# A message-passing loop whose routing work on VectorE is issued in parts of two to four operations over several steps

## The reference

```python
agg = segment_sum(feature[src] * alpha[:, None], dst)
x = x + agg @ W_fc.T + b_fc + mix(layernorm(x))
h = layernorm(x)
probs = softmax(h @ gate_w + gate_b)
idx = argmax(probs); prb = probs[idx]
one_hot = one_hot(idx, E)
pos = (cumsum(one_hot, axis=0) * one_hot).sum(-1) - 1
kept = pos < C
buf[idx, where(kept, pos, C)] = h          # then two matmuls per expert
y = ybuf[idx, min(pos, C - 1)] * prb * kept
```

## Time and profile before

| | |
|---|---|
| median of three runs | 2648.24 us (2640.82 to 2654.11) |
| span of the profiled execution, first to last instruction | 2181.3 us |
| the median less the span | 466.9 us |
| VectorE busy, whole span | 1486.4 us (68%) |
| TensorE busy | 1899.4 us (87%) |
| GpSimd busy | 1223.5 us (56%) |
| ScalarE busy | 781.6 us (36%) |
| window 1201 to 1757 us: TensorE, VectorE, GpSimd busy | 490.1, 377.4, 337.0 us of 556 |
| the same window: granted TensorE clock, DMA share | 0.90, 0.82 |
| window 1757 to 2181 us: granted TensorE clock, DMA share | 0.98, 0.54 |

### The profile page before, as it was taken

The page is one execution under the profiler, slowest core; times in us unless marked ns, Lnnn a source line. Parts: engine busy times, 40 slices in busy tenths (PEclk is TensorE's granted clock), DMA queues, the critical chain, the costliest instruction groups (busy, mean ns, idle before and its releaser), DMA issues. The chain is left out here.

```text
span 2181.3 us, 44890 instructions
## 1 busy us (share of the span) xinstructions
PE 1899.4 (87%) x12055; PEld 1346.6 (62%) x12055; DVE 1486.4 (68%) x6582; ACT 781.6 (36%) x3785; POOL 1223.5 (56%) x1251
## 2 busy tenths in 40 slices
PE   8997888878888888888887899999999679999997
PEld 5654555545555545555544566666666479999996
DVE  7775788878887888788787587666767624343433
ACT  6772444444444444444443011111111123333332
POOL 0006777777777777777774576656766312222222
PEclk9997889889888899899898799889999789999998
DMA  7867888888888888888885898877978566565650
GB/s 238 245 220 208 254 243 253 248 242 242 254 245 241 251 247 250 241 253 250 246 253 165 249 313 264 266 234 254 323 245 259 157 242 200 195 202 191 204 186 28
DMA packets 287974, 507.17 MB, mean 233 GB/s; under 512 B 59024, under 2 KB 199730, under 8 KB 287580
## 3 DMA queue, kind: packets, MB, share of 16 engines
q1 hardware_dynamic: 212556, 279.91, 40.8%
q0 software_dynamic: 75152, 224.23, 34.3%
HBM read 394.78 MB, written 112.83 MB: 233 GB/s over the span
## 5 line engine op out<-in xcount | busy, mean ns | idle before, releaser
L836 POOL DMA_INDIRECT pool_mem<-node_tab,edges x592 | 580.9, 981 | 346.1 <-issue 339.7
L1659 POOL DMA_INDIRECT main<-node_tab,edges x294 | 287.6, 978 | 189.2 <-issue 81.6
L967 PE MATMUL psum<-main 32*128 32x258 f32 x1568 | 217.3, 468 | 76.9 <-DVE main L1088 73.6
L977 PE MATMUL psum<-pool_mem,ident 128*128 128x258 f32 x592 | 201.0, 469 | 34.4 <-DMA pool_mem<-node_tab,edges 34.3
L876 ACT ACTIVATE main<-score_all,neg_max 128x8 f32<-128x8 f32 x98 | 29.6, 302 | 555.0 <-DVE neg_max L1119 555.0
L836 POOL DMA_INDIRECT main<-node_tab,edges x192 | 189.5, 987 | 58.5 <-issue 54.2
L2655 POOL DMA_INDIRECT out_dram<-pool_mem x56 | 56.9, 1016 | 282.3 <-DVE pool_mem L2752 266.6
L2685 PEld LDWEIGHTS psum<-pool_mem,main 128*128 128x128 f32 x1792 | 210.9, 194 | 3.3 <-issue 0.5
L2685 PE MATMUL psum<-pool_mem,main 128*128 128x128 f32 x1792 | 211.3, 277 | 0.1
L1000 PE MATMUL psum<-wkvT,main 128*128 128x512 f32 x392 | 200.6, 637 | 7.8 <-ACT main L886 7.5
L882 ACT ACTIVATE main<-main 128x64 f32<-128x64 f32 x784 | 197.9, 334 | 24.1 <-DVE main L1133 23.6
(11 more groups left out here) (284 smaller groups left out, 3656.8 us busy)
## 6 DMA issues: line engine op xcount, KB each, us to landing
main<-in_L_ffn_w_dram SPq DMA_DIRECT2D x64, 1024.0 KB, 5.4
main<-kept_rows SPq DMA_DIRECT2D x98, 640.0 KB
kept_rows<-pool_mem SPq DMA_DIRECT2D x74, 640.0 KB, 5.5
kept_rows<-main SPq DMA_DIRECT2D x24, 640.0 KB
node_tab<-pool_mem SPq DMA_DIRECT2D x49, 258.0 KB, 3.0
main<-proj_t SPq DMA_DIRECT2D x392, 32.2 KB
pool_mem<-node_tab,edges POOLq DMA_INDIRECT x592
moe_in<-zeros SPq DMA_DIRECT2D x32, 258.0 KB, 3.8
```

What stands on the lines that cost most here:

```text
L836: g.indirect_dma_start(source_rows(r, u, ZW + D), None, node_tab, bass.IndirectOffsetOnAxis(ap=edges[:, 0, HALF * k + u:HALF * k + u + 1], ...
L967: mm = pe.matmul(psum[:, Z_BANK[q], 0:ZW], hot_T[h][rows_q, j * P:(j + 1) * P], t_win[rows_q, h, :], start=True, stop=(pair in BY_VECTOR), ...
L977: pe.matmul(psum[:, Z_BANK[u % GROUPS_W], 0:ZW], ident[:, :], source_rows(r, u, ZW), start=False, stop=True).then_inc(s_z, 1)
L1659: g.indirect_dma_start(rows_g[k % R3][:, u - KEEP, 0:n], None, node_tab, bass.IndirectOffsetOnAxis(ap=edges[:, 0, HALF * k + u:HALF * k + ...
```

## The change

The same routing operations are placed by tables, one entry a batch, in place of fixed offsets. `route_choice` and `route_slots` take a part number; a chain's `then` becomes a wait ahead of a part and a `done` in it. The two copies of a tile leave `route_slots` and become `address`, which for batches 0 to 4 runs in the step of the tile's send.

| offsets of a batch | before, 7 tiles | batches 0 to 2 | batch 3 | batch 4 |
|---|---|---|---|---|
| `spread`, operations a step | 1, 2: six | 1 to 4: three | 1 to 3: four | 1, 2: six |
| `normalise`, `turn` | 3 to 9 | 5 to 11 | 4 to 10 | 3 to 9 |
| `route_logits` | 13 | 15 | 14 | 13 |
| `route_choice`, parts a step | 15: all | 16, 17: four | 15, 16: four | 14, 15: four |
| `rank` | 15 | 18 | 17 | 16 |
| `route_slots`, parts a step | 17: all | 19 to 22: two | 18, 19: four | 17, 18: four |
| `send` | 17 to 23 | 23 to 29 | 20 to 26 | 19 to 25 |

Batch 5 (six tiles) had spread at 1 and 2, turns from 3, logits at 12, choice and rank at 14, slots and sends from 16. It gets spread at 1 to 3, turns from 4, logits at 13, choice at 14 and 15, rank at 16, slots and sends from 17. Batches 6 and 7 keep their steps, with all parts in one. Within a VectorE step, slots now stand directly behind `spread` of the same batch, then `address`, logits and choice.

```diff
+        TURN_AT = [5, 5, 5, 4, 3, 4, 3, 3]
+        SPREAD_PARTS = [3, 3, 3, 4, 6, 4, 6, 6]
+        LOGITS_AT = [TURN_AT[b] + SIZES[b] + 3 for b in range(BATCHES)]
+        CHOICE_AT = [SIZES[b] + (9, 9, 9, 8, 7, 8, 8, 8)[b] for b in range(BATCHES)]
+        CHOICE_PARTS = [4, 4, 4, 4, 4, 4, 8, 8]
+        RANK_AT = [SIZES[b] + (11, 11, 11, 10, 9, 10, 8, 8)[b] for b in range(BATCHES)]
+        SLOTS_AT = [SIZES[b] + (12, 12, 12, 11, 10, 11, 10, 10)[b] for b in range(BATCHES)]
+        SLOTS_PARTS = [2, 2, 2, 4, 4, 8, 8, 8]
+        SEND_AT = [SIZES[b] + (16, 16, 16, 13, 12, 11, 10, 10)[b] for b in range(BATCHES)]
+        ONE_BY_ONE = 5
...
+        def parts_at(k, b, first, parts, n):
+
+            i = k - 2 * STARTS[b + 1] - first
+            return range(i * parts, min(n, (i + 1) * parts)) if i >= 0 else range(0)
...
-                    def route_choice(b):
+                    def route_choice(b, part):
...
-                        wait(v, s_re, b + 1)
-                        dve.then(v.tensor_reduce(red_n, expos_n, AX.X, ALU.add))
-                        dve.then(v.reciprocal(red_n, red_n))
+                        if part == 0:
+                            wait(v, s_re, b + 1)
+                        dve.wait()
+                        if part == 0:
+                            dve.done(v.tensor_reduce(red_n, expos_n, AX.X, ALU.add))
+                        elif part == 1:
+                            dve.done(v.reciprocal(red_n, red_n))
...
-                        for i in range(n):
-                            t = STARTS[b] + i
-                            wait(v, s_h, t + 1)
...
+                    def address(t):
+                        b = BATCH_OF[t]
+                        i = t - STARTS[b]
+                        wait(v, s_h, t + 1)
+                        v.tensor_copy(hrow[:, t % HR, D:D + 1].bitcast(I32), token_b[:, i:i + 1]).then_inc(s_rows_done, 1)
+                        v.tensor_copy(hrow[:, t % HR, D + 1:D + 2], gate_b[:, i:i + 1]).then_inc(s_rows_done, 1)
...
+                        for b in range(BATCHES):
+                            for part in parts_at(k, b, 1, SPREAD_PARTS[b], RSQRT_STEPS + 2):
+                                spread(b, part)
+                            for part in parts_at(k, b, SLOTS_AT[b], SLOTS_PARTS[b], 8):
+                                route_slots(b, part)
+                            if k == 2 * STARTS[b + 1] + SLOTS_AT[b] and b >= ONE_BY_ONE:
+                                for t in range(STARTS[b], STARTS[b + 1]):
+                                    address(t)
+                        for t in tile_at(k, SEND_AT):
+                            if BATCH_OF[t] < ONE_BY_ONE:
+                                address(t)
+                        for b in batch_at(k, LOGITS_AT):
+                            route_logits(b)
+                        for b in range(BATCHES):
+                            for part in parts_at(k, b, CHOICE_AT[b], CHOICE_PARTS[b], 8):
+                                route_choice(b, part)
```

More of the change, by code:

```diff
@@ L1449, in looked_up, with batch_at, tile_at @@
             return HALF if k < EARLY else KEEP
[L1451 to L1465, removed]
+        def batch_at(k, steps):
+            return [b for b in range(BATCHES) if 2 * STARTS[b + 1] + steps[b] == k]
+        def parts_at(k, b, first, parts, n):
+            i = k - 2 * STARTS[b + 1] - first
+            return range(i * parts, min(n, (i + 1) * parts)) if i >= 0 else range(0)
+        def tile_at(k, steps, behind=0):
+            return [STARTS[b] + i for b in range(BATCHES) for i in range(SIZES[b]) if 2 * STARTS[b + 1] + steps[b] + behind + i == k]
         def batch_logits(b):
@@ L2112, in route_choice, with route_slots @@
                             v.tensor_tensor(chosen_n, wide(expert_n), ids(n), ALU.is_equal).then_inc(s_r, 1)
-                    def route_slots(b):
+                    def route_slots(b, part):
                         n = SIZES[b]
                         chosen_n, tmp_n, prob_n, expert_n, pos_n, kept_n, trash_n, token_n, gate_n = chosen[:, 0:n, :], tmp[:, 0:n, :], prob[:, 0:n], expert[:, 0:n], pos[:, 0:n], kept_b[:, 0:n], trash_b[:, 0:n], token_b[:, 0:n], gate_b[:, 0:n]
-                        wait(v, s_rm, b + 1)
+                        if part == 0:
+                            wait(v, s_rm, b + 1)
+                        elif part == 1:
+                            wait(v, s_lgc, 2 * b + 2)
@@ L2118, in route_slots @@
                         dve.wait()
[L2119 to L2135, removed]
@@ L2186, in _ @@
                             v.tensor_copy(mixed, psum[:, MIX_BANK, :].rearrange("p (c j) -> p c j", j=D)).then_inc(s_foldc, 1)
[L2187 to L2195, removed]
+                        for b in range(BATCHES):
[6 more added lines that the diff above has]
+                                    address(t)
+                        for t in tile_at(k, SEND_AT):
+                            if BATCH_OF[t] < ONE_BY_ONE:
+                                address(t)
+                        for b in batch_at(k, LOGITS_AT):
                             route_logits(b)
-                        for b in tiled(k, 8):
-                            route_choice(b)
+                        for b in range(BATCHES):
+                            for part in parts_at(k, b, CHOICE_AT[b], CHOICE_PARTS[b], 8):
+                                route_choice(b, part)
                     chunk_table(v, dve, Arena(lo_hotT[0], HALF * P))
```

57 lines of the change are left out of this document (41 added, 16 removed).

## The result

The kernel after takes 2625.28 us (median of four runs, 2614.86 to 2628.80) against 2651.06 for the kernel before (also four). The medians are 25.8 us apart. The ratio on record, which the rest of this text uses, is 0.9885 with a 95% interval of 0.9839 to 0.9931; that is some 30 us won, 18 to 43 by the interval. Forecast were 19, at 2629.2.

A forecast was written before the change was run, and what follows sets the result against it. Bound: the message pass's TensorE-VectorE chain, broken by routing lumps. Four periods 243.2 + 2.6 + 1.7 + 4 x 7.7 = 278.3 against 298.2, 19.9 won, + 0.6 - 1.5 = 19.0, so 2629.2 us; range 2607 to 2650.

The forecast's parts named there:

- the 4.20 at the look-up: VectorE's wait for TensorE at L2024 between the choice and slots lumps, 4.20 us; forecast to be gone.
- rival C: Late plain steps: TensorE's clock falls to 1.2 GHz and stays slow into tile steps; 2671 us, chance 0.09.
- one wait of 2.07: TensorE's rank waits 2.07 us behind the choice lump; forecast to go once the rank follows the choice's end.
- Lateness grows from 5.9 to 7.7 a batch: GpSimd's moved sends delay gathers in more plain steps; 7.7 us a batch counted, four times in the sum.
- The low pace of 60.8: Message pass: a batch of seven plain and seven tile steps takes 60.8 us at the chain's undisturbed pace.
- the 64.4 of my bounds: Message pass: the least GpSimd allows a batch, seven steps at 5.32 and seven at 3.88; gives 2607.6 us.
- Rank distances of 70: Sign in the message pass: ranks of successive batches come some 70 us apart instead of 74.5.
- 0.6 won: Batch 0's square root alone, in four steps instead of two, has more room: 0.6 us won.
- 1.5 lost: Tail: batch 5's slots move to step 99, ahead of the last square root's second half; 1.5 us lost.
- every wait between two routing operations stays: VectorE's routing: no operation or wait between operations is added or removed, so its sum stays the same.
- Rival B: Nothing changes: VectorE's sum is unchanged and GpSimd, without a break wherever behind, sets the batch's time; 2648 us, chance 0.11.
- Rival A: Message pass: late gathers replace the lumps and late steps hide no routing; 6 us won, 2642 us, chance 0.18.

The follow-up runs named there:

- before again: The kernel before, unchanged, profiled once more for a second trace; 2598.11 us, one execution.
- sends_late: Kernel before with only the sends of batches 0 to 4 and their copies moved to the late steps; ratio 0.9965 to the kernel before.
- spread_lump: Kernel after with every batch's square root in two lumps of six again; ratio 0.9884 to the kernel before.
- after again: The kernel after, unchanged, profiled once more for a second trace; 2560.34 us, one execution.
- choice_alone: Kernel before with the choice of batches 0 to 4 in two steps and the rank a step behind it; ratio 0.9927 to the kernel before.

## Why the prediction came out near

- The direction, the place and the stall were right. The rank waits of batches 0 to 4 are gone (the last batch's rank, which was not changed, waits 5.7, 5.5 before again), the 4.20 at the look-up is gone, half clock in the four batches fell by 20 and 17 us, SyncE's moved loads cost nothing (VectorE waits 3.0 us for low bytes, 3.1 before again), ScalarE's little (turns wait 8.2 for it, 4.9 before again), and rival C (the clock falling in late steps) did not come: 0.91 and 0.90 against 0.88.
- The rank was under-priced as a term: I read one wait of 2.07 as a part of a lump's cost. By the ratios it is the largest single item, 14 of 30 us, and needed only one step's delay, no dividing.
- The failed step is the sends: "Lateness grows from 5.9 to 7.7 a batch", 30.8 us in the sum. It was sized on the 30.0 of gather waits in the short execution; before again has 0.2 of them, after 3.6 and sends_late 1.0, so with the ring of four the gathers are in time. Whether they would be late in an execution as short as that of the earlier trace rows no run shows. The low pace of 60.8 did not come either, and the two errors cancelled: 243.2 + 35.1 = 278.3 was forecast for four batches against 298.2, and measured were 318.2 and 310.9 against 337.7, 19.5 and 26.8 won for the 19.9 forecast. That the total came so near is luck.
- The pace was too low: as the traces read, GpSimd's least is 74 to 75 a batch, not the 64.4 of my bounds, and 60.8 lies below even those. The earlier trace rows gave the right kind of bound at the wrong size, since they come from an execution that lacked the 0.8 us in each step. Rank distances of 70 could then not be had; 80.3 came.
- Steps 16 to 30 were priced at 0.6 won; 4.6 and 8.0 came, and batch 0's square root is 3 of it by the one trace of spread_lump. The tail was priced at 1.5 lost; 4.7 and 5.0 came, some 3 of it batch 5's move. That every wait between two routing operations stays was not exact: the slots lost the one behind L2122 of before and two of their operations changed places. The slots, in parts or in a lump, cost nothing by the times, so nothing rests on it.
- Rival B said that nothing changes, since GpSimd's rate is the batch's time. GpSimd's rate looks like the floor, but before again stood 40 us above that floor; the half of B that failed is "without a break". VectorE's busy time did stay (1481.9 before again, 1481.5 after) and the time fell by 1.15%, so what counted was who waits behind the chain. For square root and slots, where nobody waits, the times show no gain from dividing. The page "VectorE: DVE Perf Modes" of the Trainium skill (section "Rules for kernel authors") asks to lower the count of chained operations, by which an unchanged count would win nothing. The runs agree with it for square root and slots and not for the choice with the rank behind it.
- Rival A asked for late gathers; 3.6 us of waits in after and 2.1 in after again speak against it.

What stays open: how the last 0.4% (choice_alone to after) divides among sends, copies and the later turns; what the rewritten code does with the old tables; and that GpSimd is the floor is read from the traces, no run made its steps shorter.

## What to carry to other kernels

Where one engine's short chain releases another, put the consumer a step behind the chain before dividing the chain: that was about half of this gain by itself. In a step with slack a lump cost nothing here; whether dividing pays in a step without slack, these runs do not resolve. Before adding up a pace, take the least of every engine per period, and check that the profiled execution's span agrees with the timed median: here a difference of a fifth was another execution, not work outside the span.

## What the runs showed of the hardware

- The kernel before ran in a span of 2181.3 us once; its runs beside the others all took 2591 to 2678 us. VectorE's look-up waits without a named releaser, 57.5 us before again, are 0 in the message pass of the short execution. In after again, at one of them, four engines that stood were released within 0.15 us, GpSimd's next gather among them:

```profile
1863.80 0.33 SPq L1596 DMA_DIRECT2D main<-kept_rows  x1
1863.80 0.37 ACT L1740 COPY pool_mem<-psum 128x256 f32<-128x256 f32 x1 [5.53 <-remote]
1863.92 0.27 DVE L2031 SCALAR_TENSOR_TENSOR pool_mem<-count,attr,psum 128x49 f32<-128x49 f32 x1 [3.02 <-remote]
1863.95 0.97 POOL L1666 DMA_INDIRECT main<-node_tab,edges  x1 [1.13 <-remote]
```

  VectorE had waited 3.02 us for a look-up that TensorE's rows show ended at 1861.2. In steps 30 to 86 of that trace, 13 of VectorE's 23 waits of 1.0 us or more for a look-up end 0.03 us ahead of a step's first gather; three of the 13 have an unknown releaser, nine name TensorE's look-up and one nothing. What holds them is not shown.
- TensorE at times starts the sixteen matmuls of a window sum singly, though no wait stands among them in the code. In after:

```profile
2005.81 1.18 PE L1838 MATMUL psum<-main,pool_mem 128*32 128x256 f32 x12
2007.76 0.59 PE L1838 MATMUL psum<-main,pool_mem 128*32 128x256 f32 x2 [0.77 <-issue]
2008.50 0.38 PE L1838 MATMUL psum<-main,pool_mem 128*32 128x256 f32 x1 [0.15 <-issue]
2009.23 0.40 PE L1838 MATMUL psum<-main,pool_mem 128*32 128x256 f32 x1 [0.35 <-issue]
```

  Groups with over 1.9 us from first to last start occur three to six times in each of the thirteen long traces, never in the short one. They come back at the same steps: at step 71 in seven of the traces, at step 7 in seven, and at step 35 in just the three that have the sends at their old steps. So they go with a place in the list of instructions; the cause is not shown.
